# Moving the squares and the normalisation of queries and keys from GpSimd to VectorE in a fused attention and expert layer

## The reference

```
xn = x / max(norm(x, axis=-1), 1e-12)        # x is q or k, 8 numbers of one head
proj = einsum('bhtd,rhdm->rbhtm', xn, omega)
feat = exp(clip(proj * sqrt(2 s) - s, -20, 20)) * constants
```

## Time and profile before

| what | value |
|---|---|
| median of 3 runs | 461.13 us |
| the profiled execution, its own time | 459.16 us |
| its span, first to last instruction | 457.4 us |
| TensorE busy | 436.7 us (95%) |
| VectorE busy | 349.6 us (76%) |
| ScalarE busy | 317.6 us (69%) |
| GpSimd busy | 192.3 us (42%) |
| mean granted TensorE clock | 0.993 |
| squares on GpSimd | 15.6 us in all, 1042 ns each |

### The profile page before, as it was taken

How to read it: one execution, slowest core, us unless ns; L and a number is a source line. 1 busy time by engine, 2 the same in 40 slices (tenths; PEclk the granted TensorE clock), 3 DMA queues, 4 the chain that set the end, 5 groups by cost and what they waited for, 6 DMA issues and landing times.

```text
span 457.4 us, 15761 instructions
## 1 busy us (share of the span) xinstructions
PE 436.7 (95%) x5720; PEld 363.9 (80%) x5720; DVE 349.6 (76%) x872; ACT 317.6 (69%) x528; POOL 192.3 (42%) x283
## 2 busy tenths in 40 slices
PE   5868999999999999999999999999999999999993
PEld 3457888888888888888888888888888888888782
DVE  6987687877878787777878787787968778667552
ACT  4338686786868587786868678586866858686761
POOL 5725444343544434444543443454344345434210
PEclk9989999999999999999999999999999999999998
DMA  3401103020200202020020202002020201103000
GB/s 84 108 24 24 28 12 59 14 48 26 48 19 6 57 11 52 17 46 23 3 54 11 57 11 46 23 15 42 11 57 11 46 11 34 24 1 59 4 12 12
DMA packets 45243, 14.37 MB, mean 31 GB/s; under 512 B 35328, under 2 KB 45056, under 8 KB 45216
## 3 DMA queue, kind: packets, MB, share of 16 engines
q1 hardware_dynamic: 44512, 13.54, 14.4%
q10 hardware_dynamic: 576, 0.46, 0.3%
q0 software_dynamic: 128, 0.01, 0.1%
HBM read 3.44 MB, written 2.10 MB: 12 GB/s over the span
## 4 chain that ended last, share of the span: by engine, by line
PE 87%; DVE 6%; ACT 2%; issue 2%; DMA 1%; POOL 1%; DVEq 0%; ACTq 0%; POOLq 0%
PE x L959 18%; PE p_s L1009 9%; PE p_t L1009 7%; PE x L1158 7%; PE x L1167 7%; PE x L1126 7%; PE x L1179 6%; PE p_s L1022 5%; PE x L1022 4%; PE x L1099 3%; PE p_s L994 2%; PE x L1110 2%; PE x L1063 2%; PE x L1075 2%; DMA weight_c<-L_attn_quad_weights_dram 1%
## 5 line engine op out<-in xcount | busy, mean ns | idle before, releaser
L466 POOL TENSOR_TENSOR s_sb<-s_sb,causal 128x256 f32<-128x256 f32 x96 | 68.4, 734 | 88.7 <-ACT s_sb L559 88.7
L553 ACT ACTIVATE feat<-arg,f_bias 128x1024 f32<-128x1024 f32 x64 | 71.7, 1147 | 10.2 <-DVE arg L768 10.2
L768 DVE TENSOR_SCALAR arg<-p_s,f_low,f_high 128x1024 f32<-128x1024 f32 x32 | 42.8, 1338 | 15.5 <-PE p_s L994 10.9
L1009 PEld LDWEIGHTS p_s<-feat 64*64 64x64 f32 x1024 | 39.2, 133 | 16.0 <-issue 14.3
L315 POOL TENSOR_TENSOR qk_sq<-qkv 128x512 f32<-128x512 f32 x15 | 15.6, 1042 | 83.6 <-DVE qkv L745 83.6
L1009 PE MATMUL p_s<-feat 64*64 64x256 f32 (+3 forms) x1024 | 50.1, 311 | 0.0
L460 POOL TENSOR_TENSOR s_sb<-s_sb,causal 128x512 f32<-128x512 f32 x30 | 37.6, 1276 | 26.7 <-ACT s_sb L565 26.7
L1009 PE MATMUL p_t<-feat 64*64 64x256 f32 (+3 forms) x1024 | 47.1, 299 | 0.0
L768 DVE TENSOR_SCALAR arg<-p_t,f_low,f_high 128x1024 f32<-128x1024 f32 x32 | 42.7, 1333 | 0.0
L1009 PEld LDWEIGHTS p_t<-feat 64*64 64x64 f32 x1024 | 41.4, 134 | 1.5
L559 ACT ACTIVATE s_sb<-p_s 128x384 f32<-128x384 f32 x48 | 23.6, 491 | 19.6 <-PE p_s L1009 19.6
(11 more groups left out here) (152 smaller groups left out, 1043.5 us busy)
## 6 DMA issues: line engine op xcount, KB each, us to landing
out_dram<-out_sb SPq DMA_DIRECT2D x32, 64.0 KB, 2.1
xin<-in_L_attn_x_dram SPq DMA_DIRECT2D x31, 64.0 KB, 2.3
se_rows<-n_L_ffn_slot_embeds_dram SPq DMA_DIRECT2D x1, 256.0 KB, 3.2
w_f<-in_L_ffn_w_dram SPq DMA_DIRECT2D x1, 256.0 KB, 4.0
w_sb<-in_L_ffn_w_dram SPq DMA_DIRECT2D x1, 256.0 KB, 3.9
stack_t<-stack SPq DMA_TRANSPOSE x16, 4.3
wqkv_f<-in_L_attn_Wqkv_dram ACTq DMA_DIRECT2D x1, 192.0 KB, 4.0
bqkv_bc<-in_L_attn_bqkv_dram ACTq DMA_DIRECT2D x1, 192.0 KB, 6.7
```

Source lines behind the costliest of these rows:

```text
L466: pool.tensor_tensor(v, v, m, ALU.mult).then_inc(mb_ok, 1)
L553: nc.scalar.activation(feat[:, k:k + 2, :], arg[:, k:k + 2, :], ACT.Exp, bias=f_bias[:, 0:1]).then_inc(fe_ok, 1)
L768: nc.vector.tensor_scalar(arg[:, k:k + 2, :], (p_s, p_t)[g % 2][:, :, :], f_low[:, 0:1], f_high[:, 0:1], ALU.max, ALU.min).then_inc(cl_ok, 1)
L1009: mm = nc.tensor.matmul(dst[rows:rows + 64, u, o:o + hi - lo], f[:, T + keys:T + keys + 64], f[:, lo:hi], start=True, stop=True, skip_grou ...
```

## The change

`squares` and `qk_apply` for the next row leave GpSimd's list. On VectorE `squares` is put directly behind `qkv_bias` and ahead of `evac_a` 0, and `qk_apply` directly behind `qk_newton` and ahead of `ln_newton`. Semaphores, tiles and all other orders stay.

```diff
@@ pool row
                 if nxt:
                     residual(b1)
-                    squares(pool, b1)
                 mask_b(b, 0)
                 mask_b(b, 1)
                 if nxt:
-                    qk_apply(pool, b1)
                     stack_low(pool, b1)
@@ dve row
                 if nxt:
                     qkv_bias(b1)
+                    squares(dve, b1)
                 evac_a(b, 0)
                 evac_a(b, 1)
...
                 evac_a(b, 3)
                 if nxt:
                     qk_newton(b1)
+                    qk_apply(dve, b1)
                 if nxt2:
                     ln_newton(b2)
```

## The result

The changed kernel takes 473.12 us in the median of 4 runs (472.92 to 473.38), the kernel before 460.48 us in the median of its 4 (457.99 to 461.27). The ratio is 1.0298, with a 95% interval of 1.0268 to 1.0329: slower by 3%. The profiled executions took 473.21 and 459.16 us, with spans of 471.5 and 457.4.

What follows compares the result with a forecast made beforehand. TensorE looked full but was paced by VectorE's floor, through root, table load and gelu to `processed_low`. 8 x 0.98 + 6 x 1.06 = 14.2 us on 459.16 gave 473.4, put at 475 us for a median; range 465.5 to 480.

Steps and rivals of the forecast that it cites:

- they end after the mask's end: VectorE's squares, held by GpSimd's mask 0 in rows 1 to 14, end 0.56 us after it.
- `evac_a` 0 late: First evacuation behind the held squares on VectorE starts 1.32 us later in row 8, 1.24 in row 7.
- the floor's record shorter: VectorE's floor, with mask 1 done long before, gives back 0.26 us.
- logarithm late: ScalarE's logarithm of `qk_root`, waiting for the floor, is 1.06 us late in rows like 8.
- `processed_low` late: TensorE's `processed_low` in row 8, released by the gelu, is late by the logarithm's 1.06 us.
- row 7 longer: Odd rows and row 14, eight rows, each lose 0.98 us through the late floor and logarithm.
- `qk_apply`: Its move to VectorE, between `qk_newton` and `ln_newton`, costs nothing; without cover between -0.02 and 0.85 us a row.
- row 0: Squares fit into VectorE's wait for `scores` 0 and the masks do not meet them: no cost.
- sum: Rows 1 to 14 together: 8 x 0.98 + 6 x 1.06 = 14.2 us slower.
- Rival 1: Squares not held by the mask: 0.53 us in 14 rows, 7.4 us; chance 0.26 including held in odd rows alone.
- Rival 2: Not slower: `evac_b` 2, not the floor, holds the logarithm; at best 2 us faster; chance 0.09.
- Rival 3: TensorE's and the gelu's delays before `processed_low` add: 7.7 us more; chance 0.05, shared with another delay.

Runs made afterwards that it cites:

- x1: Kernel before with only `qk_apply` moved to VectorE, squares staying on GpSimd: 459.92 us, ratio 1.0021.
- x5: Changed kernel with the logarithm of `qk_root` reading a constant, not waiting for the floor; true lengths left out in rows 1 to 15: 468.32 us, ratio 1.0200.
- x7: Kernel before with the logarithm reading a constant, not waiting for the floor; true lengths left out in rows 1 to 15: 457.62 us, ratio 0.9973.
- x3: Changed kernel with GpSimd's mask 0 waiting for the squares on VectorE: 466.76 us, ratio 1.0186.
- x6: x5 with GpSimd's mask 0 also waiting for the squares: 461.75 us, ratio 1.0054.
- x9d: Kernel before with `qk_apply` on VectorE, masks 0 and 1 behind the floor, `evac_b` 2 behind first gelu, `stack_high` behind second: 453.41 us, ratio 0.9885.
- x4: Changed kernel with the squares on VectorE placed behind `slots_low`, directly ahead of `qk_norms`: 469.16 us, ratio 1.0232.
- x2: Kernel before with only the squares moved to VectorE, `qk_apply` staying on GpSimd: 473.27 us, ratio 1.0336.
- x8: Kernel before with `qk_apply` on VectorE, masks 0 and 1 behind the floor, `evac_b` 2 behind the first gelu: 459.91 us, ratio 1.0028.

## Why the prediction was right

The prediction was 475 us for a median and 473.4 against the profiled execution's own time; measured were 473.12 and 473.21. The mechanism is borne out step by step; the 2 us that I put on top for a median are not. I added them because the median of before lay above its profiled execution, but the four runs of the changed kernel took 472.92 to 473.38. Step by step, in row 8:

| step | predicted | measured |
|---|---|---|
| squares are ready after the bias's end | 0.10 us | 0.11 (252.53 to 252.64) |
| they end after the mask's end | 0.56 | 0.56; row 7 0.54 |
| `evac_a` 0 late | 1.32; row 7 1.24 | 1.33; 1.24 |
| the floor's record shorter | 0.26 | 0.26 |
| logarithm late | 1.06 | 1.07 (4.84 against 3.77 from the bias) |
| `processed_low` late | 1.06 | 1.07 (7.78 against 6.71) |
| row 7 longer | 0.98 | 0.98 (27.43 against 26.45) |
| `qk_apply` | 0 | x1: 1.0021, interval from 0.9999 |
| row 0 | 0 | 26.75 us from row 0 to row 1, 26.72 before |
| sum | 14.2 us | span 14.1, execution 14.05 |

**What bounds.** The claim on which all rests was that a TensorE with 342.98 of 343.36 us busy was not at its own limit, but paced by the floor on VectorE. x5 to x7 bear it out: by the ratios, a logarithm that does not wait for the floor takes the loss from 13.7 to 9.2 us, where the late `evac_a` 0 is next, and with the masks held from 8.5 (x3) to 2.5 (x6). Since the same logarithm takes 1.2 us off the kernel before as well, the part that does not go over the floor is 10.7 us in x5 and 4.1 in x6 (their medians against x7's): the two delays lie beside each other, as forecast, and without the floor the shorter one sets the row. x9d is the direct sign that TensorE was not at its limit: the same matmuls take 26.12 us a row instead of 26.41.

**The hold.** The rows had shown a VectorE operation on 4 elements held by GpSimd. x3 shows that it applies to 512, and x4 that the one that starts first wins, by as little as 0.01 us in the records, and that the other waits for the whole instruction, on either engine. That agrees with the rule that the prediction took from the Trainium skill, SBUF — State Buffer, section Who interferes with whom. Rival 1 (7.4 us) is what x3 came to, 7.9 us by the medians: it is the price of the squares without the collision. The collision costs the other 6 us or so (6.5 between x2 and x3).

**What was off, without consequence.** I put `scores` 2 late by 0.55 us in row 8; it is late by 0.75 (from 2.42 to 3.17 after the bias's start), because the release of the `hold` takes 0.24 and not 0.05. TensorE is then ready for `processed_low` at 258.72, and the gelu releases it at 259.18, so 0.46 us of cover were left where the prediction had 0.65 (251.57 to 252.22). That this error cost nothing is luck of the sum: it lies beside the longer delay. The same mistake is what x5 and x6 laid open.

Rival 2 (not slower) needed squares below 0.26 us; they cost at least 0.79 with their wait. Rival 3 (both delays add) did not occur; by the table the longer alone counts.

The median of before in the first comparison was 460.48, so that of the 14.2 us forecast 12.6 are left between the medians; the single runs of before spread over 3 us, those of the changed kernel over 0.5. Against the medians of before in the later runs, 458.75 to 458.84, the difference is 14.3.

## What to carry to other kernels

An engine that is 100% busy in the records can still be paced by another: look whether its first instruction behind a wait comes right after the releaser, and compare with a row where the wait is not binding (here row 15, which prepares no next row). Before work is moved to VectorE, look what GpSimd will do at that very moment: an operation with both inputs in SBUF that came 0.08 to 0.16 us behind a GpSimd multiply waited here for the whole of it. The floor, an operation with one tile as input, was held as well: 0.46 us beside mask 1, 0.20 without it. Work that is off the path on a slow engine, here 1.04 us of squares on GpSimd, is cheaper than 0.69 us on the path. And when a stall is taken away, look where it goes: in x8 it moved from the first gelu to the second.

## What was not expected of the hardware

- The release of the matmuls of `scores` 2, behind two waits on instructions of their own, took 0.24 to 0.25 us; that of `processed_low`, by a wait without such an instruction, 0.05. The transposition in x8, also without one, took 0.15 (252.66 to 252.81). What makes the difference was not tried by itself.
- A held VectorE multiply of 512 elements ends 0.54 to 0.56 us after GpSimd's instruction, 0.13 to 0.15 less than its length alone of 0.69, as the prediction had taken from 4 elements.
- To take a late start of 0.14 to 0.18 us out of TensorE's list gave 0.29 us a row. A part of it is the group behind the stall, which ran for 1.78 us instead of 1.90, as in row 15 of the kernel before; the cause of that was not tried by itself.
